# Maxima that read their scale row from a PSUM bank, made chunk by chunk, and the odd tile of each pair of paste sums made by GpSimd

## What is computed

```
f = b[:, :, ::2, ::2]                                  # 40x40
w = patches(f, 3, 1)                                   # L x 576
wn = w / max(sqrt(sum(w*w)), 1e-4)
yi = einsum('bpd,bld->blp', w, wn) * mm                # L x L scores
yi = softmax(yi * 10, axis=1) * mm
patches = einsum('blp,bld->bpd', yi, raw_w)            # raw_w: 4x4 patches, stride 2
out = overlap-add of the 4x4 patches / 4
```

## Time and profile before

| | us |
|---|---|
| median of 3 runs | 1367.72 |
| lowest, highest | 1367.48, 1370.94 |
| the profiled execution, its own time | 1372.19 |
| its span, first to last instruction | 1370.4 |
| PE, DVE, ACT, POOL busy | 1194.4, 1169.1, 994.5, 584.3 |
| granted TensorE clock, mean | 0.966 |

### The profile page before, as it was taken

One profiled execution on the slowest core, in us unless ns is written; L12 is line 12 of the kernel. 1 busy time (PEld: TensorE's weight loads), 2 busy tenths in 40 slices (PEclk: granted clock), 3 DMA queues, 4 the chain that ended last, 5 costly groups with the idle time before them and its releaser, 6 DMA issues.

```text
span 1370.4 us, 20011 instructions
## 1 busy us (share of the span) xinstructions
PE 1194.4 (87%) x4910; PEld 750.1 (55%) x4910; DVE 1169.1 (85%) x2315; ACT 994.5 (73%) x2881; POOL 584.3 (43%) x510
## 2 busy tenths in 40 slices
PE   4785988979888889989899899988899889897896
PEld 3555654656546655565556555566555655465443
DVE  4576999889998899879998899988998799988872
ACT  2888676886778868796768877787777967687331
POOL 1002543346442554336442464425643365334772
PEclk9887999999999999999999999999999999999898
DMA  5311344335353353443444353533534434432442
GB/s 80 44 36 46 100 120 110 89 94 138 89 128 87 99 129 97 115 104 100 124 107 98 96 137 96 126 84 97 137 91 114 111 94 115 106 85 83 136 141 55
DMA packets 179175, 138.36 MB, mean 101 GB/s; under 512 B 119602, under 2 KB 177010, under 8 KB 179058
## 3 DMA queue, kind: packets, MB, share of 16 engines
q1 hardware_dynamic: 178898, 136.57, 39.2%
q10 hardware_dynamic: 160, 0.50, 0.2%
HBM read 19.76 MB, written 13.11 MB: 24 GB/s over the span
## 4 chain that ended last, share of the span: by engine, by line
DVE 43%; PE 21%; issue 17%; ACT 14%; SPq 2%; DMA 2%; DVEq 1%; POOL 1%; ACTq 0%; POOLq 0%
PE psO L586 12%; DVE S L1039 10%; DVE G L1102 9%; DVE Z L1126 8%; PE psG L534 6%; DVE G L999 6%; ACT S L808 5%; DVE G L994 3%; ACT G L727 2%; ACT G L819 2%; PE psG L549 1%; DVE Z L1123 1%; DVE Z L1122 1%; DMA SH<-G 1%; SPq L388 1%
## 5 line engine op out<-in xcount | busy, mean ns | idle before, releaser
L1243 POOL TENSOR_TENSOR G<-G,SH 123x492 f32<-123x492 f32 (+1 forms) x448 | 548.1, 1232 | 768.9 <-DMA SH<-G 766.3
L586 PE MATMUL psO<-Z,B 123*128 123x492 f32 (+2 forms) x1792 | 720.8, 533 | 73.8 <-DVE Z L1126 61.0
L586 PEld LDWEIGHTS psO<-Z,B 123*128 123x128 f32 x1792 | 336.3, 195 | 291.1 <-issue 142.1
L1039 DVE CUSTOM_DVE_ANT_0 S<-G,RB 123x492 f32<-123x492 f32 (+1 forms) x448 | 346.1, 784 | 18.5 <-ACT G L727 18.1
L819 ACT ACTIVATE G<-G,nb 123x492 f32<-123x492 f32 (+1 forms) x448 | 268.3, 642 | 128.5 <-DVE G L1102 126.9
L808 ACT ACTIVATE S<-S,nm 123x480 f32<-123x480 f32 (+3 forms) x560 | 309.1, 554 | 7.1
L534 PE MATMUL psG<-LH,HL 128*123 128x492 f16 (+2 forms) x1104 | 275.9, 359 | 32.0 <-ACT G L727 20.8
L1102 DVE SCALAR_TENSOR_TENSOR G<-G,RA,psB 123x492 f32<-123x492 f32 (+1 forms) x448 | 269.8, 644 | 0.4 <-PE psB L469 0.4
L1126 DVE TENSOR_TENSOR Z<-G 123x984 f32<-123x984 f32 (+2 forms) x192 | 230.5, 1200 | 29.3 <-POOL G L1243 27.6
L534 PEld LDWEIGHTS psG<-LH,HL 128*123 128x123 f16 x1104 | 144.4, 138 | 147.0 <-issue 64.8
L534 PE MATMUL psG<-H 128*123 128x492 f16 (+2 forms) x368 | 130.3, 354 | 0.0
(11 more groups left out here) (85 smaller groups left out, 748.0 us busy)
## 6 DMA issues: line engine op xcount, KB each, us to landing
SH<-G SPq DMA_DIRECT2D x336, 214.8 KB
SH<-G SPq DMA_DIRECT2D x112, 89.2 KB
SH<-G SPq DMA_DIRECT2D x336, 19.2 KB
XP<-x SPq DMA_DIRECT2D x20, 280.0 KB, 4.2
XP<-mid SPq DMA_DIRECT2D x20, 280.0 KB, 4.1
HL<-LH SPq DMA_DIRECT2D x16, 246.5 KB, 3.7
mid<-OSB SPq DMA_DIRECT2D x48, 80.0 KB, 2.4
out<-OSB SPq DMA_DIRECT2D x48, 80.0 KB, 2.3
```

The source lines that it names most:

```text
L586: last = pe.matmul(psO[:, b, 0:n], B[:, o:o + 128], Z[:, 2 * (s % 2) + j, 0:n], start=t == 0, stop=t == TILES - 1)
L1039: dve.tensor_tensor_reduce(S[:, slot, 0:n], G[:, g:g + n], RB[:, s0 * TW:s0 * TW + n], 1.0, 0.0, ALU.mult, ALU.max, mx[:, slot:slot + 1]). ...
L1243: pool.tensor_tensor(g, g, SH[:, o % SFREE, 0:n], ALU.add).then_inc(y1_made, 1)
```

## The change

1. **No RB, no ACT copy.** `scale_rows(v, k)` on PE now spreads the scales of score chunk `k` into a bank of their own, psR, and `maxima` reads psR as its first input and the tile of G as its second. ACT's `scale_rows` is gone, and so is R (the column RA, which was made beside it, is used). The number of spread columns is what it was.
2. **Chunk by chunk.** The spread of chunk `k` stands on PE behind `second_half` of the chunk's first score pair, and waits until all maxima of the chunk before are made, since there is one bank. For this the second maximum of a chunk's last pair (`AT_ONCE`: 6, 13, 20, 27, and 22) is made in its own slot and not in the next.
3. **One bank for lse rows.** psL takes the place of the two banks: the row of chunk `k` is spread at the end of slots 2, 9 and 16 behind the paste, after all arguments of the chunk before; it stood at slots 2, 5 and 10.
4. **Odd tiles of Z on POOL.** `sum_even` on DVE makes the first tile of a pair and waits for one shifted tile fewer; `sum_odd` on POOL makes the second, ahead of `add_shifted` in each slot, and counts `odd_z_made`. PE waits for it ahead of the second tile's paste; ACT and DVE wait for it, besides Z, before they write G's columns again.

```diff
-            def scale_rows(u, v, g):
+            def scale_rows(v, k):
                 pe.wait_ge(r_step, (v + 1) * R_STEPS)
...
+                    pe.wait_ge(max_made, v * NB + k * TILES)
+                s0, n = S_CHUNKS[k]
+                spread(psR[0:TW, :], RA, v * TILES + s0, v * TILES + s0 + n).then_inc(r_rows, 1)
...
+                    pe.wait_ge(arg_made, v * NB + k * TILES)
                 s0, n = P_CHUNKS[k]
-                spread(psB[0:TW, k % 2, :], lse, s0, s0 + n).then_inc(lse_rows, 1)
+                spread(psL[0:TW, :], lse, s0, s0 + n).then_inc(lse_rows, 1)
...
+                else:
+                    pe.wait_ge(odd_z_made, u * SLOTS + k * PAIRS + i + 1)
...
+                    if pairs and pairs[0] % PAIRS == 0:
+                        scale_rows(v, pairs[0] // PAIRS)
...
-            def scale_rows(v, g):
-                act.wait_ge(r_psum, v * 4 + g + 1)
-                n = min(4, TILES - 4 * g) * TW
-                act.activation(RB[:, 4 * g * TW:4 * g * TW + n], ROW_BANK[g][:, 0:n], ACT.Copy).then_inc(r_rows, 1)
...
-                dve.tensor_tensor_reduce(S[:, slot, 0:n], G[:, g:g + n], RB[:, s0 * TW:s0 * TW + n], 1.0, 0.0,
+                dve.tensor_tensor_reduce(S[:, slot, 0:n], psR[0:TW, 0:n], G[:, g:g + n], 1.0, 0.0,
                                          ALU.mult, ALU.max, mx[:, slot:slot + 1]).then_inc(max_made, 1)
...
-                dve.wait_ge(y1_made, u * NB + k * TILES + min(2 * i + 3, TILES) + SFREE)
+                dve.wait_ge(y1_made, u * NB + k * TILES + 2 * i + 2 + SFREE)
...
-                    dve.tensor_tensor(Z[:, slot:slot + 2, 0:n], g[:, 2 * i:2 * i + 2, c0:c0 + n],
-                                      g[:, 2 * i - 1:2 * i + 1, c0 - TW:c0 - TW + n], ALU.add).then_inc(z_made, 1)
+                tile = G[:, 2 * i * GLEN + c0:2 * i * GLEN + c0 + n]
+                above = (2 * i - 1) * GLEN + c0 - TW
+                dve.tensor_tensor(Z[:, slot, 0:n], tile, G[:, above:above + n] if i else SHJ[:, 0:n],
+                                  ALU.add).then_inc(z_made, 1)
...
+            def sum_odd(at, s):
+                u, k, i = at
+                c0, n = z_cols(k)
+                pool.wait_ge(y1_made, u * NB + k * TILES + min(2 * i + 3, TILES) + SFREE)
...
+                pool.wait_ge(z_used, u * SLOTS + k * PAIRS + i + 1)
+                tile, above = (2 * i + 1) * GLEN + c0, 2 * i * GLEN + c0 - TW
+                pool.tensor_tensor(Z[:, 2 * (s % 2) + 1, 0:n], G[:, tile:tile + n], G[:, above:above + n],
+                                   ALU.add).then_inc(odd_z_made, 1)
...
             def body(u, v):
                 for s in BODY:
+                    at = place(u, v, s + 1)
+                    if at:
+                        sum_odd(at, s + 1)
```

More of the change, by code:

```diff
@@ L189, in contextual_attention @@
         psO = ps("psO", [128, 2, 512])
-        psB = ps("psB", [128, 2, 512])
+        psL = ps("psL", [128, 512])
+        psR = ps("psR", [128, 512])
         psM = ps("psM", [128, 512])
@@ L453, in row_squares @@
                 pe.sem_inc(pe_gate, 1)
-                if v is not None:
-                    pe.wait_ge(r_rows, v * 4 + 3)
+                if v:
+                    pe.wait_ge(b_made, v * PAIRS)
                 for r in range(FROWS // 2):
@@ L594, in body @@
                     pairs = score_list(s) if v is not None else []
-                    if s == 4 and v is not None:
-                        scale_rows(u, v, 2)
-                    if s == 18 and v is not None:
-                        scale_rows(u, v, 3)
-                    if s == 5 and u is not None:
-                        lse_row(u, v, 2)
-                    if s == 10 and u is not None:
-                        lse_row(u, v, 3)
                     if s == FIRST and v is not None:
@@ L624, in body @@
                     if s == 24 and v is not None:
-                        lse_row(v, w, 0)
-                    if s == FIRST and u is not None:
-                        lse_row(u, v, 1)
+                        lse_row(v, 0)
+                    if u is not None and s % PAIRS == FIRST and s // PAIRS < NK - 1:
+                        lse_row(u, s // PAIRS + 1)
                     if w is not None:
@@ L634, in body @@
                         block_group(v, w, s - 21)
-                    if w is not None and s in (25, 26):
-                        scale_rows(u, w, s - 25)
             pe.wait_ge(mask_step, 2)
@@ L878, in body @@
                         softmax_pair(at)
-                    if s == 4 and v is not None:
-                        scale_rows(v, 2)
-                    if s == 18 and v is not None:
-                        scale_rows(v, 3)
                     if w is not None:
@@ L1021, in maxima @@
                 n = w * TW
-                if i == 0 and par == 0 and k != 1:
-                    dve.wait_ge(r_rows, v * 4 + max(k + 1, 2))
+                if i == 0 and par == 0:
+                    dve.wait_ge(r_rows, v * NK + k + 1)
                     dve.sem_inc(dve_gate, 1)
@@ L1045, in score_pair @@
                 next(adds, None)
-                if j - 1 not in (-1, 22):
+                if j and j - 1 not in AT_ONCE:
                     maxima(v, j - 1, 1)
@@ L1102, in argument_pair, with sum_even @@
                     dve.scalar_tensor_tensor(out=g, in0=g, scalar=RA[:, bass.ds(u * TILES + t, 1)],
-                                             in1=psB[0:TW, k % 2, 0:n],
+                                             in1=psL[0:TW, 0:n],
                                              op0=ALU.mult, op1=ALU.subtract).then_inc(arg_made, 1)
-            def sum_pair(at, s):
+            def sum_even(at, s):
                 u, k, i = at
@@ L1206, in _ @@
             squared_norms(0)
-            scales(None, 0)
+            scales(0)
             body(None, 0, 1)
```

67 lines of the change are left out of this document (23 added, 44 removed).

## The result

The changed kernel takes 1277.9 us (median of 4 runs, 1276.3 to 1282.7) against 1369.3 for the kernel before beside it. The ratio is 0.9336, 95% interval 0.9301 to 0.937: 91 us less, where 48 were forecast and the range ended at 1285. The sign was right, the size was not.

The account below looks back on a forecast made before the run. It took a near tie of PE and DVE as the bound, with PE alone on top afterwards. 1372.2 - 49 (full units) - 2 (first body) + 7 - 4 (last unit) = 1324, or 1320 us as median; 8-in-10 range 1285 to 1360.

Parts of the forecast that it names:

- DVE's time: DVE's busy time: -75.5 us for maxima, -142 for odd sums, +63 for contention, together -155, 19 a unit.
- loss per remaining two-input instruction: On DVE, contention with GpSimd per instruction with two SBUF inputs, scaled from 0.18 to 0.26 us; +63 us in all.
- GpSimd's 832: GpSimd's busy time in us, forecast to rise from 584 by 248 for the 224 odd sums.
- full units: Seven units with both pastes and scores: from 160 to 153 us each, -49 us in all.
- first body: The stretch without pastes at the start: four copies less on ACT, -2 us.
- last unit: The unit without scores: GpSimd leads in 14 wide slots, +7 us; shorter waits for shifted tiles and GpSimd, -4.
- new waits: At chunk turns (slots 9, 16, 22), maxima wait for PE's spread and PE for old maxima: +3 us a unit, bounds 0 and 7.
- the floor: In a full unit, PE's busy time of 147 us plus turns between chunks remains: 150 us, -10 a unit.
- Rival (A): PE has less work than its busy time says; a unit falls to about 147 us, total 1278; chance 0.15.
- (B): New waits at chunk turns of 7 to 9 us a unit eat the gain: 1355 us or no change; chance 0.12.
- (C): GpSimd's in-order queue, held by DVE, becomes the pace: some 1466 us, or 1399 with a third of that; chance 0.07.
- (D): The maxima's PSUM operand brings nothing; DVE falls by 80 us only, gain 4 a unit, 1340 us; chance 0.08.

Follow-up runs that it names:

- odd sums alone: The kernel before with only the odd sums moved to GpSimd; RB, ACT's copies and both lse banks stay: 1359.6 us, ratio 0.9965.
- maxima alone: The changed kernel with the joint sums back on DVE, so maxima from psR chunk by chunk and the single lse bank stay: 1303.9 us, ratio 0.9554.
- the fills: The kernel before with 224 unread 384-column DVE fills, behind each paste sum (1406.4 us) or, in another run, behind each score pair's first maximum (1398.7 us).

## Why the prediction was right in sign and wrong in size

- **DVE's time: right.** -155 us forecast, -158 measured; maxima at 664 and 406 ns, even sums dearer by contention. The maxima brought 82.7 us where 75.5 were taken, so a part of the closeness is that misses cancel. The loss per remaining two-input instruction was taken as 0.26 us; the 96 even sums of 492 columns lost 0.42 each and the 72 narrow L972 0.17, which balances. GpSimd's 832 was too high by 60, since it is held less as well.
- **Where the miss lies.** The sum came to 1324 for the profiled execution, and it took 1279.3: 45 us. Of these 37 lie in the full units (-49 forecast, -86 measured), 4 in the first body and 4 in the last unit. In a full unit, 150 us plus 3 of new waits were forecast and 147.3 came out. So two steps of the prediction failed, the floor (2.7 us a unit, 19 in all) and the new waits (3 us a unit, 21); the kernel before had 159.6 us a unit where 160 was taken, which is 3 us the other way.
- **The floor, what DVE's time is worth: wrong.** I took PE's busy time, 147 us a unit, as the floor, added a turn of 1 us a chunk, and came to 150 to 151. The full units came to 147.3. Three things were wrong in it. The 147 was read from one unit, 460 to 620 us, which has the highest of the seven: they go from 143.2 to 147.0, mean 144.9. PE's busy time is also no fixed amount of work: in the changed kernel the seven have a mean of 140.8, with the same matmuls, and 19 of the 27 us that it fell by over the full units are the stretches at half clock, which came behind PE's own waits. And added work didn't add time: PE took 67 us more of matmuls in the kernel before at 2 to 3 us of time.
- **Rival (A)** had this, with a chance of 0.15, and its 1278 is the measured time. Its mechanism was named by half, without the clock, and the hit is in part luck: it set a unit equal to PE's busy time of 147, where PE is busy 141 of 147.3 us and idle for the rest.
- **The new waits: wrong, +3 us a unit forecast, no cost seen.** They exist, 25.5 us of DVE's idle time for psR, within the 20 to 40 expected, 8.0 for psL, and 8.9 on PE. But without the turns the kernel is no faster, and with DVE's wait for psR halved it is the same. I had costed in full a delay on an engine for which I had just worked out 23 us a unit of room.
- **The first body: -2 forecast, -6 measured.** Its mean granted clock was 0.89 over 137 us before and 0.92 over 131 now, so about 15 and 10 us of work at full speed lost. That could be most of the difference, but no run tried it.
- **The last unit: +3 forecast, -1 measured.** GpSimd leads in the wide slots as said, 27.0 of 27 us in one chunk, which took 25 before. That the odd sums there cost nothing against sums on DVE was not foreseen. DVE still waited 20.8 us for GpSimd's shifted adds and PE 9.1 for its odd sums, all in this unit, so the -4 for shorter waits has little in the rows for it.
- **The other rivals.** (B), new waits that eat the gain, and (C), GpSimd as pace, didn't come about in the full units. (D) is refuted by the maxima's rows. The rule that a VectorE instruction with two SBUF inputs contends with a GpSimd instruction that reads SBUF (the Trainium skill, "SBUF — State Buffer", "Who interferes with whom") is borne out by one operand moved: 915 ns to 664 in the same order. In its strict reading, every even sum waiting for a whole odd one, it was too hard: 0.42 us lost of 1.23.
- **What stays open.** DVE's busy time doesn't order the runs by itself: -37 us brought 5 (odd sums alone) and -76 brought 61 (maxima alone), where a rise of 49 by the fills cost 31 to 40. At the fills' rate, 0.6 to 0.8, the 76 would be worth 47 to 62 and the 37 some 23 to 30. So it is the odd sums in the old order that brought less than their share, and no run says why. The granted clock goes the same way: the maxima alone gave back 20 us of it, the odd sums alone 3. ACT's copies, 12.6 us by the run that puts them back, are also in the 61. How the 61 part among operand, copies, order and clock was only argued.

## What to carry to other kernels

Before an engine's busy time is taken as the floor, add a little work to it: if the time doesn't move, it isn't one, and its busy time may shrink with its waits. Where VectorE and GpSimd run side by side, look first at which VectorE instructions have two SBUF inputs; giving the most frequent one a PSUM operand, which also did away with its copies, brought 61 us here, more than the 5 to 30 of work moved to GpSimd, and this work paid more with it (26 to 30 us) than without it in the same order (13 to 16). A few waits on an engine with room cost nothing here, but room is no free space for work: filling 10.6 us a unit of DVE's cost about 4. Both are better tried than summed.

## What the runs showed of the hardware

- A custom multiply-and-maximum of 492 columns took 664 ns in the mean and 673 at most with its first input in PSUM and one in SBUF, with GpSimd busy 43% of the span as with 60%. With both in SBUF it took about 0.67 us alone; its mean was 806 and 832 ns with GpSimd busy 43% and 42%, and 861 and 915 with 59% and 58%.
- At slot 9 of a unit PE was idle for about half of 4 us, 2.12 us of it at a stretch, and then ran 3.4 us at 1.2 GHz, although it was busy for the whole of that time. Filling that idle time in each unit with matmuls that nobody reads made the kernel 5 us faster.
- GpSimd's adds got shorter too when the maxima's second SBUF input went, in the same order of work: at 205 columns from 799 to 682 ns with the odd sums on GpSimd, and from 732 to 665 without them.
